# First attention with one set of row statistics ahead of its loop; expert sums scattered into two arrays that are joined at the end, with six buffers for gathered rows

## The chip, the cores and the metric

One core of one Trainium2 chip runs the whole program in one launch. The metric is device time in microseconds (us); lower is better. An engine is called PE (TensorE), PEld (its weight loads), DVE (VectorE), ACT (ScalarE), POOL (GpSimd) or SP (SyncE, which only issues DMAs here).

## The reference, cut to what matters

The input x has 64 sequences of 64 rows of 256 f32 values: T = 4096 rows, held as NT = 32 tiles of 128 rows (two sequences each). Four layers follow one another, each of the form x = x + layer(layernorm(x)):

1. a cross-attention with 32 heads of 8 and rotary positions, on a context of 128 values per row;
2. a feed-forward that keeps half of the rows;
3. a second cross-attention with 16 heads of 16;
4. a mixture of 64 experts, 8 chosen per row, at most 64 rows per expert:

```
w, sel = top_k(softmax(x @ gate_w.T), 8);  w = w / sum(w)
xin[e, slot] = x[token]                       (slot < 64, later ones are dropped)
h = silu(xin @ wg[e]) * (xin @ wu[e])
y[token] += (h @ wd[e]) * w                   (every expert adds to its rows)
```

## The kernel before, in words

All data is f32. x stays in SBUF (`k.xres`) through the first three layers. Each layer is a stage with a barrier at its end, and in each stage every engine runs its own list of instructions, tied to the others by semaphores.

**First attention** (`first_attention`). SP issues the constants, a first part of x, the weights, the keys and values of tiles 0 and 1, and then the rest of x. x comes in six parts, `X_PARTS`, of 4, 4, 6, 6, 6 and 6 tiles. DVE takes the layernorm statistics of part 0 alone (`part_statistics(0)`: one `bn_stats` per tile at L469, then five small operations at L108 to L114 for the part), ACT makes the scale (L121, L123), DVE the shift (L129), and the loop over the tiles begins. The loop is a software pipeline of depth 5: step n normalises tile n (L485), makes its query and key (L364, L365), and works on tiles n-1 to n-4 at later points (scores L292 with the maximum and the subtraction L490 and L494 on DVE; transposes L304, exponentials L411, products with the values L316; output L382, residual L509). `pipelined` writes the first steps out (6 on PE and POOL; 8 on ACT and DVE, by `PEEL`) and runs the rest as a loop. On DVE steps 1 to 5 each end with `part_statistics(n)` for the next part of x, ahead of step n+1's normalisation in DVE's order. SP puts three later loads (weights of the other layers) behind the key and value loads of each of tiles 2 to 13.

**Route and slots** (`route`, `fill_slots`). The rows are normalised again, gated, and stored with their 64 expert weights as a table of rows of 320 values in DRAM (`table`, L1151); x itself is stored into `out` (L1147), in eight groups of four tiles. `fill_slots` then finds each expert's rows, with DVE alone busy for most of it.

**Experts** (`experts`). 64 experts are worked through as 32 pairs, two pairs to a batch: 16 batches (`NB_E`). Of each pair, POOL gathers 128 rows of the table by an indirect DMA (L1414) into one of `GOT_E` = 4 buffers of a batch each. PE turns them (L1444), multiplies (L1470), turns the hidden values (L1486), multiplies again (L1459), and sums rows that both experts of a pair hold with a matmul (L1479); ACT copies the result to `add`, which has two buffers (L1508). POOL scatters the 128 rows of a pair into `out` by an indirect DMA that adds (L1428). The adding reads and writes rows that another pair may hit too, so each scatter waits until the one before it has landed (`e_added`). POOL's order is: scatter of pair 0, gather of pair 0 of batch n+3, scatter of pair 1, gather of pair 1 of batch n+3. SP loads the weights of eight batches ahead, 1.125 MiB per batch (768 KB and 384 KB), until batch 7 has been worked through.

Of the kernel before, what the change touches and what calls it, by code (L numbers as in the profile page):

```python
# [6 lines left out]
F32 = mybir.dt.float32  # L7
U32 = mybir.dt.uint32
ALU = mybir.AluOpType
# [3 lines left out]
P = 128  # L13
# [39 lines left out]
GOT_E = 4  # L53
# [4 lines left out]
def pipelined(eng, step, tiles, depth, peel=0):  # L58

    first = max(depth + depth % 2, peel)
# [38 lines left out]
def row_statistics(dve, k, done, tiles=slice(0, NT), before=0):  # L104

    raw = k.raw[:, tiles, :]
    mean2, apart, square = k.mean2[:, tiles], k.apart[:, tiles], k.square[:, tiles]
    dve.tensor_tensor(mean2, raw[:, :, 1], raw[:, :, 4], ALU.add).then_inc(done, 1)  # L108
    dve.tensor_tensor(apart, raw[:, :, 1], raw[:, :, 4], ALU.subtract).then_inc(done, 1)
    dve.tensor_tensor(square, raw[:, :, 2], raw[:, :, 5], ALU.add).then_inc(done, 1)  # L110
    dve.wait_ge(done, 5 * before + 2)
    dve.scalar_tensor_tensor(out=k.spread2[:, tiles], in0=apart, scalar=0.25, in1=apart, op0=ALU.mult, op1=ALU.mult).then_inc(done, 1)
    dve.wait_ge(done, 5 * before + 4)
    dve.scalar_tensor_tensor(out=k.var[:, tiles], in0=square, scalar=1.0 / D, in1=k.spread2[:, tiles],  # L114
                             op0=ALU.mult, op1=ALU.add).then_inc(done, 1)


def row_scales(act, k, statistics_done, ln_done, scale_done, tiles=slice(0, NT), before=0):

    act.wait_ge(statistics_done, 5 * before + 5)  # L120
    act.activation(k.lnv[:, tiles], k.var[:, tiles], ACT.Ln, bias=k.ln_eps[:, 0:1]).then_inc(ln_done, 1)  # L121
    act.wait_ge(ln_done, before + 1)
    act.activation(k.rstd[:, tiles], k.lnv[:, tiles], ACT.Exp, scale=-0.5).then_inc(scale_done, 1)  # L123


def row_shifts(dve, k, scale_done, shift_done, tiles=slice(0, NT), before=0):

    dve.wait_ge(scale_done, before + 1)
    dve.scalar_tensor_tensor(out=k.nmr[:, tiles], in0=k.mean2[:, tiles], scalar=-0.5, in1=k.rstd[:, tiles],  # L129
                             op0=ALU.mult, op1=ALU.mult).then_inc(shift_done, 1)  # L130
    dve.wait_ge(shift_done, before + 1)
# [27 lines left out]
def first_attention(nc, ins, k, bank):  # L159

    with ExitStack() as stack:
# [24 lines left out]
        (a_const, a_weights, a_xin0, a_xin1, a_xin2, a_xin3, a_xin4, a_xin5, a_keys0, a_keys1, a_vals0, a_vals1, a_fill, a_ang, a_turns,  # L186
# [4 lines left out]
             "a_const a_weights a_xin0 a_xin1 a_xin2 a_xin3 a_xin4 a_xin5 a_keys0 a_keys1 a_vals0 a_vals1 a_fill a_ang a_turns "  # L191
# [3 lines left out]
        x_in, keys_done, vals_done = [a_xin0, a_xin1, a_xin2, a_xin3, a_xin4, a_xin5], [a_keys0, a_keys1], [a_vals0, a_vals1]  # L195
# [3 lines left out]
        PEEL = 8  # L199
        X_PARTS = [slice(0, 4), slice(4, 8), slice(8, 14), slice(14, 20), slice(20, 26), slice(26, NT)]  # L200
# [14 lines left out]
        def _(sp):  # L215
            def load_x(c):
                sp.dma_start(k.xres[:, X_PARTS[c], :], x_rows[:, X_PARTS[c], :]).then_inc(x_in[c], 16)

# [170 lines left out]
        def _(act):  # L389
# [9 lines left out]
            row_scales(act, k, a_stats, a_lnv_done, a_rstd_done, X_PARTS[0])  # L399

            def step(n, i, u, on):
                t, tk, a, w, f = n, n - 1, n - 2, n - 3, n - 4
                v = 1 - u
                if isinstance(n, int) and 2 <= n <= len(X_PARTS):
                    row_scales(act, k, a_stats, a_lnv_done, a_rstd_done, X_PARTS[n - 1], n - 1)

# [39 lines left out]
            pipelined(act, step, NT, DEPTH, PEEL)  # L446

        @block.vector
        def _(dve):
# [15 lines left out]

            def part_statistics(c):
                dve.wait_ge(x_in[c], 16)
                for t in range(X_PARTS[c].start, X_PARTS[c].stop):
                    dve.bn_stats(tile_of(k.raw, t), tile_of(k.xres, t)).then_inc(a_raw, 1)  # L469
                dve.wait_ge(a_raw, X_PARTS[c].stop)  # L470
                row_statistics(dve, k, a_stats, X_PARTS[c], c)

            part_statistics(0)
            row_shifts(dve, k, a_rstd_done, a_nmr_done, X_PARTS[0])
            dve.wait_ge(a_table, 4)

            def step(n, i, u, on):
                t, a, w, f = n, n - 2, n - 3, n - 4
                v = 1 - u
                if isinstance(n, int) and 3 <= n <= len(X_PARTS) + 1:  # L480
                    row_shifts(dve, k, a_rstd_done, a_nmr_done, X_PARTS[n - 2], n - 2)
# [617 lines left out]
def route(nc, ins, k, bank, out, table):  # L1099
# [4 lines left out]
    with ExitStack() as stack:  # L1104
# [34 lines left out]
        def _(sp):  # L1139
# [3 lines left out]
            sp.dma_start(table[T:T + P, :], zero[:, :]).then_inc(r_pad, 16)  # L1143
            for g in range(groups):
# [9 lines left out]
            sp.wait_ge(r_pad, 32)  # L1154
# [219 lines left out]
def experts(nc, ins, k, bank, out, table):  # L1374

    with ExitStack() as stack:
# [13 lines left out]
        (e_idx_s, e_got0, e_got1, e_got2, e_got3, e_gotT, e_gotTc, e_row, e_twin_s, e_again_s, e_shift_s, e_to_s,  # L1390
         e_gu, e_silu, e_hid_s, e_hidT, e_hidTc, e_y, e_part_s, e_sum, e_add_s, e_added
         ) = z.sems(
             "e_idx_s e_got0 e_got1 e_got2 e_got3 e_gotT e_gotTc e_row e_twin_s e_again_s e_shift_s e_to_s "
             "e_gu e_silu e_hid_s e_hidT e_hidTc e_y e_part_s e_sum e_add_s e_added")
        got_in = [e_got0, e_got1, e_got2, e_got3]
# [13 lines left out]
        def _(pool):  # L1409
# [12 lines left out]
            for n in range(NB_E):  # L1422
                pool.wait_ge(e_to_s, n + 1)
                pool.wait_ge(e_add_s, n + 1)
                for p in range(2):
                    if n or p:
                        pool.wait_ge(e_added, 16 * (2 * n + p))
                    pool.indirect_dma_start(out=out[:, :], out_offset=bass.IndirectOffsetOnAxis(ap=to[:, n, p:p + 1], axis=0),  # L1428
                                            in_=add[:, n % 2, p, :], in_offset=None, compute_op=ALU.add).then_inc(e_added, 16)
# [60 lines left out]
        def _(act):  # L1490
            act.preload_act_table(ACT.Silu)
            for n in range(NB_E + 1):
# [65 lines left out]
def program(nc, ins, out, table):  # L1558
    with ExitStack() as stack:
# [52 lines left out]
        with nc.sbuf_tensor("found", [P, T // 2], F32) as found:  # L1612
            k.found = found
            route(nc, ins, k, bank, out, table)
            fill_slots(nc, ins, k, bank)
        experts(nc, ins, k, bank, out, table)
# [73 lines left out]
```

## Time and profile before

| | before |
|---|---|
| time, median of 3 runs | 1127.8 us (1126.14 to 1131.03) |
| the profiled execution's own time | 1132.87 us |
| its span (first to last instruction) | 1131.1 us |
| busy: PE / DVE / ACT / POOL | 903.2 / 662.7 / 426.4 / 334.1 us |
| mean granted clock of TensorE | 0.887 |
| DMA traffic | 56.28 MB |

The span is what the trace shows; 1.8 us of the execution's time lie around it. A busy share is a mean over stages with different limits, so the stages are read one by one. "xn" below is the normalised tile, and the start of its instruction on DVE marks the start of a step in the first attention.

### The profile page before, as it was taken

What the parts mean: (1) busy time and instruction counts of PE and PEld (TensorE: products, weight loads), DVE (VectorE), ACT (ScalarE), POOL (GpSimd) and SP (SyncE); (2) the same over time, 40 slices, a digit from 0 to 9 for tenths busy, and PEclk for the clock granted to TensorE, in tenths of its full rate; (3) what the DMA queues carried; (4) which work ended last, traced back from release to release, by engine and by line L of the source; (5) the groups of instructions that cost most, each with busy time, mean ns of one, the idle gap of its engine ahead of it and who ended that gap; (6) DMA issues with size and microseconds to landing.
All of it is one profiled execution on the core that took longest, in us unless ns stands there. A gap on an engine that the chain in (4) does not pass through costs nothing. (4 is left out here: it accounts for less than half of the span.)

```text
span 1131.1 us, 25460 instructions
## 1 busy us (share of the span) xinstructions
PE 903.2 (80%) x9176; PEld 693.5 (61%) x9176; DVE 662.7 (59%) x1481; ACT 426.4 (38%) x1013; POOL 334.1 (30%) x293
## 2 busy tenths in 40 slices
PE   4789999999998599998699999999977600655661
PEld 2567777777776598897467777777746500433440
DVE  4756777777775455553377677776742586333331
ACT  2324444444443223333266655656537400221220
POOL 3313333433441200000333333333410101344552
PEclk9678999999999699999699999999985655788886
DMA  6311100000000000000101100001003592567342
GB/s 196 94 35 33 27 14 14 14 14 14 14 9 4 1 1 0 0 0 1 17 16 17 16 14 14 14 16 17 12 1 113 195 297 93 137 174 188 63 68 24
DMA packets 74395, 56.28 MB, mean 50 GB/s; under 512 B 40689, under 2 KB 69489, under 8 KB 74353
## 3 DMA queue, kind: packets, MB, share of 16 engines
q1 hardware_dynamic: 68208, 46.29, 14.0%
q0 software_dynamic: 6144, 9.44, 4.9%
q8 instruction: 25, 0.41, 0.2%
q14 instruction: 18, 0.14, 0.0%
HBM read 41.78 MB, written 13.93 MB: 49 GB/s over the span
## 5 line engine op out<-in xcount | busy, mean ns | idle before, releaser
L411 ACT ACTIVATE pr_t<-bank 128x512 f32<-128x512 f32 x128 | 76.3, 596 | 159.7 <-PE bank L304 159.0
L837 POOL TENSOR_TENSOR g_k_bd<-g_k_t,head_mask 128x1024 f32<-128x1024 f32 x32 | 60.6, 1893 | 133.3 <-ACT g_k_t L1016 133.3
L316 PEld LDWEIGHTS bank<-v_bd,pr_t 128*64 128x64 f32 x2048 | 73.1, 142 | 27.8 <-issue 27.6
L304 PE MATMUL bank<-ident,sub 128*128 128x128 f32 x512 | 86.3, 293 | 3.0 <-ACT pr_t L411 2.3
L316 PE MATMUL bank<-v_bd,pr_t 128*64 128x18 f32 x2048 | 86.0, 217 | 0.1
L304 PEld LDWEIGHTS bank<-ident,sub 128*128 128x128 f32 x512 | 59.7, 147 | 29.6 <-issue 18.6
L494 DVE TENSOR_TENSOR sub<-bank,top 128x2048 f32<-128x2048 f32 x32 | 73.3, 2291 | 3.7
L264 POOL TENSOR_TENSOR rot<-part_a,part_b 128x512 f32<-128x512 f32 x32 | 40.6, 1268 | 116.9 <-DVE part_b L503 116.9
L655 ACT ACTIVATE f_hid<-bank,b 128x128 f32<-128x128 f32 x128 | 36.5, 368 | 97.7 <-PE bank L600 97.7
L490 DVE TENSOR_REDUCE top<-bank 128x32 f32<-128x2048 f32 x32 | 73.1, 2284 | 0.3
L1428 POOL DMA_INDIRECT out<-e_add,e_to x32 | 50.7, 1583 | 75.0 <-DMA out<-e_add,e_to 57.2
L272 POOL TENSOR_TENSOR k_bd<-qk_t,head_mask 128x1024 f32<-128x1024 f32 x32 | 60.6, 1893 | 33.0 <-ACT qk_t L426 33.0
L600 PE MATMUL bank<-f_xs_t,w 128*128 128x128 f32 x512 | 64.5, 280 | 0.0
L600 PEld LDWEIGHTS bank<-f_xs_t,w 128*128 128x128 f32 x512 | 60.4, 194 | 5.1 <-ACT f_hid L655 5.0
L636 PE MATMUL bank<-w,f_hid 128*128 128x256 f32 x256 | 57.9, 379 | 0.0
L986 ACT ACTIVATE g_sq<-g_qk 128x512 f32<-128x512 f32 x32 | 20.2, 630 | 86.9 <-DVE g_qk L1091 86.9
L503 DVE TENSOR_TENSOR part_a<-bank,cos_t 128x512 f32<-128x512 f32 x32 | 22.1, 692 | 52.0 <-PE bank L365 52.0
L636 PEld LDWEIGHTS bank<-w,f_hid 128*128 128x128 f32 x256 | 47.4, 190 | 5.8
L1524 DVE COPY e_part<-bank 128x512 f32<-128x512 f32 x16 | 11.1, 691 | 67.7 <-PE bank L1459 67.7
L1414 POOL DMA_INDIRECT e_got<-table,e_idx x32 | 31.6, 988 | 62.4 <-DVE e_idx L1517 52.9
L1444 PE MATMUL bank<-ident,e_got 128*128 128x128 f32 x64 | 12.3, 322 | 46.1 <-DMA e_got<-table,e_idx 46.1
L980 ACT ACTIVATE g_pr_t<-bank 128x512 f32<-128x512 f32 x64 | 38.2, 597 | 19.1 <-PE bank L881 18.4
(192 smaller groups left out, 2073.8 us busy)
## 6 DMA issues: line engine op xcount, KB each, us to landing
e_w_gu<-in_experts_in SPq DMA_DIRECT2D x16, 768.0 KB, 5.4
e_w_d<-in_experts_out SPq DMA_DIRECT2D x16, 384.0 KB, 6.4
table<-r_row SPq DMA_DIRECT2D x16, 320.0 KB, 2.9
out<-xres SPq DMA_DIRECT2D x16, 256.0 KB, 3.3
xres<-in_x SPq DMA_DIRECT2D x4, 768.0 KB, 9.8
keys_in<-in_ctx_t SPq DMA_DIRECT2D x32, 64.0 KB, 1.9
vals_in<-in_ctx_t SPq DMA_DIRECT2D x32, 64.0 KB, 1.8
w<-in_L_ffn_w SPq DMA_DIRECT2D x2, 1024.0 KB, 6.8
```

The costliest lines, as they stand in the source:

```text
L264: pool.tensor_tensor(rot[:, v, :], part_a[:, v, :], part_b[:, v, :], ALU.add).then_inc(a_rot, 1)
L272: pool.tensor_tensor(k_bd[:, v, :, :, :, :].rearrange("p c b h s -> p (c b) h s"), qk_t[:, v, KC:2 * KC, :].rearrange("p c (b a s) -> p (c ...
L304: m = pe.transpose(b_pr[:, j * P:(j + 1) * P], sub[:, v, cols], k.ident[:, :])
L316: m = pe.matmul(b_o[64 * b:64 * b + 64, hp * VW0:(hp + 1) * VW0], pr_t[:, e, j, b * S:(b + 1) * S], v_bd[:, v, b, hp, :], start=True, stop ...
L411: act.activation(pr_t[:, e, :, :].rearrange("p j q -> p (j q)"), b_pr[:, :], ACT.Exp).then_inc(a_exp, 1)
L490: dve.tensor_reduce(top[:, :], sc, AX.X, ALU.max).then_inc(a_top, 1)
L494: dve.tensor_tensor(sub[:, u, :].rearrange("p (h s) -> p h s", s=S), sc, stretch(top[:, :], S), ALU.subtract).then_inc(a_sub, 1)
L600: mm = pe.matmul(b_h[half][:, (c % 4) * P:(c % 4 + 1) * P], k.w1[:, d, c * P:(c + 1) * P], xs_t[:, u, d, :], start=(d == 0), stop=(d == KC ...
L636: mm = pe.matmul(b_y[:, 0:D], hid[:, u, c, :], k.w2[:, c, :], start=(c == 0), stop=(c == FC - 1))
L837: pool.tensor_tensor(k_bd[:, v, :, :, :, :].rearrange("p c b h s -> p (c b) h s"), k_t[:, v, :, :].rearrange("p c (b a s) -> p (c b) a s", ...
L980: act.activation(pr_t[:, e, :, :].rearrange("p j q -> p (j q)"), b_pr[:, :], ACT.Exp).then_inc(g_exp, 1)
L1428: pool.indirect_dma_start(out=out[:, :], out_offset=bass.IndirectOffsetOnAxis(ap=to[:, n, p:p + 1], axis=0), in_=add[:, n % 2, p, :], in_o ...
```

## The change: what it does

It has two parts that share no code.

**First attention.** x comes in four parts of eight tiles (1 MB each). DVE takes the statistics of all 32 tiles ahead of the first step (four small loops over `bn_stats`, then the five operations, the scale and the shift once, 32 columns wide). No step has statistics in it any more. `PEEL` goes, so that ACT and DVE write out six steps as the others do. All 30 later loads stand right behind x in SP's list, ahead of the keys and values of tile 2.

**Experts.** The scatter of pair 0 of a batch adds to `out`, that of pair 1 to a new DRAM array `extra`; each waits only for the scatter before it on the same array. Both are issued, then the two gathers, now of batch n+5, since `GOT_E` is 6. At the end four DMAs of POOL add `extra` to `out`, DRAM to DRAM, 1 MB each. `extra` has to be zero first: `route` fills it with nine DMAs, 4.3 MB, ahead of its other stores in SP's list.

```
-GOT_E = 4
+GOT_E = 6
...
-            for c in range(1, len(X_PARTS)):
+            for c in range(1, PARTS):
                 load_x(c)
-            ahead, share = 14, -(-len(k.later_loads) // 12)
-            for t in range(2, ahead):
-                both(t, t // 2, t % 2)
-                for dst, src in k.later_loads[(t - 2) * share:(t - 1) * share]:
-                    sp.dma_start(dst, src).then_inc(k.loaded, 16)
-            with sp.Fori(ahead // 2, NT // 2) as i:
+            for dst, src in k.later_loads:
+                sp.dma_start(dst, src).then_inc(k.loaded, 16)
+            with sp.Fori(1, NT // 2) as i:
...
-            part_statistics(0)
-            row_shifts(dve, k, a_rstd_done, a_nmr_done, X_PARTS[0])
+            for c, part_in in enumerate(x_in):
+                dve.wait_ge(part_in, 16)
+                with dve.Fori(c * NT // PARTS, (c + 1) * NT // PARTS) as t:
                     dve.bn_stats(tile_of(k.raw, t), tile_of(k.xres, t)).then_inc(a_raw, 1)
+            dve.wait_ge(a_raw, NT)
+            row_statistics(dve, k, a_stats)
+            row_shifts(dve, k, a_rstd_done, a_nmr_done)
...
-                if isinstance(n, int) and 1 <= n < len(X_PARTS):
-                    part_statistics(n)
-            pipelined(dve, step, NT, DEPTH, PEEL)
+            pipelined(dve, step, NT, DEPTH)
...
+            for c in range(NT // 4):
+                sp.dma_start(extra[4 * P * c:4 * P * (c + 1), :].rearrange("(t p) d -> p t d", p=P),
+                             spread(zero[:, 0:D], 4)).then_inc(r_pad, 16)
+            sp.dma_start(extra[T:T + P, :], zero[:, 0:D]).then_inc(r_pad, 16)
...
-                for p in range(2):
-                    if n or p:
-                        pool.wait_ge(e_added, 16 * (2 * n + p))
-                    pool.indirect_dma_start(out=out[:, :], ..., compute_op=ALU.add).then_inc(e_added, 16)
-                    if n + GOT_E - 1 < NB_E:
-                        gather(n + GOT_E - 1, p)
-            pool.wait_ge(e_added, 32 * NB_E)
+                for p, sum_of, landed in ((0, out, e_added), (1, extra, e_extra)):
+                    if n:
+                        pool.wait_ge(landed, 16 * n)
+                    pool.indirect_dma_start(out=sum_of[:, :], ..., compute_op=ALU.add).then_inc(landed, 16)
+                for p in range(2):
+                    if n + GOT_E - 1 < NB_E:
+                        gather(n + GOT_E - 1, p)
+            pool.wait_ge(e_added, 16 * NB_E)
+            pool.wait_ge(e_extra, 16 * NB_E)
+            for c in range(4):
+                rows = slice(c * T // 4, (c + 1) * T // 4)
+                pool.dma_start(out=out[rows, :]..., in_=extra[rows, :]...,
+                               accum_op=ALU.add, max_dma_last_dim=8192).then_inc(e_joined, 16)
+            pool.wait_ge(e_joined, 64)
...
-                        act.wait_ge(e_added, 32 * (n - 2))
+                        act.wait_ge(e_added, 16 * (n - 2))
+                        act.wait_ge(e_extra, 16 * (n - 2))
```

DVE in step 2 of the first attention, from its normalisation to that of step 3, before (`raw`, `mean`, `apart`, `square`, `spread`, `var` are the statistics, `nmr` the shift, `sub` the scores less their maximum):

```order
L485 TENSOR_SCALAR xn<-xres,rstd,nmr 128x256
L490 TENSOR_REDUCE top<-bank 128x32
L494 TENSOR_TENSOR sub<-bank,top 128x2048
L503 TENSOR_TENSOR part_a<-bank,cos_t 128x512
L503 TENSOR_TENSOR part_b<-bank,sin_t 128x512
L469 BN_STATS raw<-xres 128x6 x6
L108 TENSOR_TENSOR mean<-raw 128x6
L109 TENSOR_TENSOR apart<-raw 128x6
L110 TENSOR_TENSOR square<-raw 128x6
L112 SCALAR_TENSOR_TENSOR spread<-apart 128x6
L114 SCALAR_TENSOR_TENSOR var<-square,spread 128x6
L129 SCALAR_TENSOR_TENSOR nmr<-mean,rstd 128x4
```

The same place in the changed kernel, where its lines have other numbers:

```order
L475 TENSOR_SCALAR xn<-xres,rstd,nmr 128x256
L480 TENSOR_REDUCE top<-bank 128x32
L484 TENSOR_TENSOR sub<-bank,top 128x2048
L493 TENSOR_TENSOR part_a<-bank,cos_t 128x512
L493 TENSOR_TENSOR part_b<-bank,sin_t 128x512
L475 TENSOR_SCALAR xn<-xres,rstd,nmr 128x256
```

The twelve instructions of the statistics that stood between two normalisations are gone from the step; they stand ahead of step 0 now, for all tiles.

POOL at the start of the experts, before (`e_got` are the gathered rows, `e_add` the rows to be added, `e_idx` and `e_to` the row numbers):

```order
L1414 DMA e_got<-table,e_idx 128x320 x6
L1428 DMA out<-e_add,e_to 4224x256
L1414 DMA e_got<-table,e_idx 128x320
L1428 DMA out<-e_add,e_to 4224x256
L1414 DMA e_got<-table,e_idx 128x320
```

and in the changed kernel, its start and its end:

```order
L1406 DMA e_got<-table,e_idx 128x320 x10
L1420 DMA out<-e_add,e_to 4224x256
L1420 DMA extra<-e_add,e_to 4224x256
L1406 DMA e_got<-table,e_idx 128x320 x2
...
L1420 DMA out<-e_add,e_to 4224x256
L1420 DMA extra<-e_add,e_to 4224x256
L1429 DMA out<-extra 128x2048 x4
```

The two scatters of a batch stand side by side, the gathers behind both, ten gathers instead of six come before the first scatter, and the four joining DMAs (128 rows of 2048 values, 8 KB, each) come last.

## Rows read from the trace of the kernel before

**Rows 1.** The page, granted clock of TensorE in 40 slices of 28 us.

```profile
PEclk9678999999999699999699999999985655788886
```

**Rows 2.** DVE's timeline (start us, us, instruction): step starts in the first attention.

```profile
9.69 0.41 DVE L485 TENSOR_SCALAR xn<-xres,rstd,nmr 128x256 f32<-128x256 f32 x1
...
15.62 0.40 DVE L485 TENSOR_SCALAR xn<-xres,rstd,nmr 128x256 f32<-128x256 f32 x1
...
25.21 0.41 DVE L485 TENSOR_SCALAR xn<-xres,rstd,nmr 128x256 f32<-128x256 f32 x1
...
84.12 0.41 DVE L485 TENSOR_SCALAR xn<-xres,rstd,nmr 128x256 f32<-128x256 f32 x1
...
98.42 0.41 DVE L485 TENSOR_SCALAR xn<-xres,rstd,nmr 128x256 f32<-128x256 f32 x1
...
108.03 0.41 DVE L485 TENSOR_SCALAR xn<-xres,rstd,nmr 128x256 f32 x1
```

**Rows 3.** Timeline at the end of step 5: statistics on DVE, then PE's wait.

```profile
81.29 2.05 DVE L469 BATCH_NORM_STATS2 raw<-xres 128x6 f32<-128x256 f32 x6
...
84.67 0.69 PE L332 MATMUL bank<-ident,xn 128*128 128x128 f32 x2 [2.67 <-DVE xn L485]
```

**Rows 4.** PE's timeline, the query product in step 6 and in step 7.

```profile
90.92 2.07 PE L364 MATMUL bank<-wq,xn_t 128*128 128x256 f32 x4
...
102.44 1.13 PE L364 MATMUL bank<-wq,xn_t 128*128 128x256 f32 x4
```

**Rows 5.** Windows (us; busy PE, PEld, DVE, ACT, POOL; clock, DMA share, GB/s).

```profile
20.00:24.00 4.00, 3.41 (x37) 1.77 (x35) 1.97 (x5) 0.00 (x0) 1.52 (x2) 1.00 0.15 50
```

**Rows 6.** Windows in the second attention, whose first step starts at 540.86.

```profile
540.00:550.00 10.00, 5.59 (x14) 3.19 (x14) 3.13 (x6) 1.84 (x5) 2.67 (x6) 0.50 0.09 14
...
560.00:570.00 10.00, 7.96 (x90) 5.70 (x90) 6.03 (x11) 6.05 (x14) 2.62 (x2) 1.00 0.14 23
```

**Rows 7.** POOL's timeline in the experts: first, middle and last scatters.

```profile
974.43 1.62 POOL L1428 DMA_INDIRECT out<-e_add,e_to  x1 [11.10 <-ACT e_add L1508]
...
1036.49 1.59 POOL L1428 DMA_INDIRECT out<-e_add,e_to  x1 [3.32 <-DMA out<-e_add,e_to]
...
1038.39 0.98 POOL L1414 DMA_INDIRECT e_got<-table,e_idx  x1 [0.30 <-issue]
...
1040.60 1.59 POOL L1428 DMA_INDIRECT out<-e_add,e_to  x1 [1.23 <-DMA out<-e_add,e_to]
...
1046.69 1.59 POOL L1428 DMA_INDIRECT out<-e_add,e_to  x1 [3.22 <-DMA out<-e_add,e_to]
...
1121.04 1.55 POOL L1428 DMA_INDIRECT out<-e_add,e_to  x1 [2.49 <-DMA out<-e_add,e_to]
```

**Rows 8.** The chain that ended last: the scatter before the last, from issue to landing.

```profile
1117.00 3.78 DMA out<-e_add,e_to
```

**Rows 9.** The page, costliest groups (count, busy us, mean ns, idle before): the scatters.

```profile
L1428 POOL DMA_INDIRECT out<-e_add,e_to x32 | 50.7, 1583 | 75.0 <-DMA out<-e_add,e_to 57.2
```

**Rows 10.** PE's timeline, turning gathered rows and hidden values in the first batches.

```profile
967.04 0.60 PE L1444 MATMUL bank<-ident,e_got 128*128 128x128 f32 x4
...
973.95 0.60 PE L1444 MATMUL bank<-ident,e_got 128*128 128x128 f32 x4
...
978.91 0.42 PE L1486 MATMUL bank<-ident,e_hid 128*96 128x128 f32 x2 [0.75 <-DVE e_hid L1532]
```

**Rows 11.** Windows: weight loads alone; experts with weight loads; one scatter alone.

```profile
910.00:930.00 20.00, 0.00 (x0) 0.00 (x0) 19.73 (x13) 0.00 (x0) 0.00 (x0) 0.50 0.97 314
1035.00:1045.00 10.00, 6.30 (x36) 3.94 (x36) 3.12 (x12) 1.90 (x4) 5.14 (x4) 0.83 0.64 168
1112.20:1116.90 4.70, 0.00 (x0) 0.00 (x0) 0.00 (x0) 0.00 (x0) 1.55 (x1) 0.50 0.25 28
```

**Rows 12.** SP's timeline in the route stage: the first stores of x, the first of the table.

```profile
848.72 0.98 SPq L1147 DMA_DIRECT2D out<-xres  x2
867.78 0.88 SPq L1151 DMA_DIRECT2D table<-r_row  x2
```

More of the change, by code:

```diff
@@ L52, with pipelined @@
 RING_E = 8
-GOT_E = 4
+GOT_E = 6
 GT = 4
 ROWS_R = 4
-def pipelined(eng, step, tiles, depth, peel=0):
-    first = max(depth + depth % 2, peel)
+def pipelined(eng, step, tiles, depth):
+    first = depth + depth % 2
     def peeled(n):
@@ L101, in stretch @@
     return ap.rearrange("p (h a) -> p h a", a=1).to_broadcast([ap.shape[0], ap.shape[1], n])
[L104 to L114, printed above, removed]
-                             op0=ALU.mult, op1=ALU.add).then_inc(done, 1)
@@ L118, in row_scales, with row_statistics @@
[L118 to L129, printed above, removed]
+def row_statistics(dve, k, done):
+    mean_e, mean_o = k.raw[:, :, 1], k.raw[:, :, 4]
+    dve.tensor_tensor(k.mean2[:, :], mean_e, mean_o, ALU.add).then_inc(done, 1)
+    dve.tensor_tensor(k.apart[:, :], mean_e, mean_o, ALU.subtract).then_inc(done, 1)
+    dve.tensor_tensor(k.square[:, :], k.raw[:, :, 2], k.raw[:, :, 5], ALU.add).then_inc(done, 1)
+    dve.wait_ge(done, 2)
+    dve.scalar_tensor_tensor(out=k.spread2[:, :], in0=k.apart[:, :], scalar=0.25, in1=k.apart[:, :],
+                             op0=ALU.mult, op1=ALU.mult).then_inc(done, 1)
+    dve.wait_ge(done, 4)
+    dve.scalar_tensor_tensor(out=k.var[:, :], in0=k.square[:, :], scalar=1.0 / D, in1=k.spread2[:, :],
+                             op0=ALU.mult, op1=ALU.add).then_inc(done, 1)
@@ L130, in row_shifts, with row_scales @@
+def row_scales(act, k, statistics_done, ln_done, scale_done):
+    act.wait_ge(statistics_done, 5)
+    act.activation(k.lnv[:, :], k.var[:, :], ACT.Ln, bias=k.ln_eps[:, 0:1]).then_inc(ln_done, 1)
+    act.wait_ge(ln_done, 1)
+    act.activation(k.rstd[:, :], k.lnv[:, :], ACT.Exp, scale=-0.5).then_inc(scale_done, 1)
+def row_shifts(dve, k, scale_done, shift_done):
+    dve.wait_ge(scale_done, 1)
+    dve.scalar_tensor_tensor(out=k.nmr[:, :], in0=k.mean2[:, :], scalar=-0.5, in1=k.rstd[:, :],
                              op0=ALU.mult, op1=ALU.mult).then_inc(shift_done, 1)
-    dve.wait_ge(shift_done, before + 1)
+    dve.wait_ge(shift_done, 1)
@@ L445, in step @@
                                    ACT.Copy).then_inc(a_attTc, 1)
-            pipelined(act, step, NT, DEPTH, PEEL)
+            pipelined(act, step, NT, DEPTH)
         @block.vector
@@ L1095, in second_attention, with route @@
         z.end()
-def route(nc, ins, k, bank, out, table):
+def route(nc, ins, k, bank, out, extra, table):
     with ExitStack() as stack:
@@ L1370, in fill_slots, with experts @@
         z.end()
-def experts(nc, ins, k, bank, out, table):
+def experts(nc, ins, k, bank, out, extra, table):
     with ExitStack() as stack:
@@ L1555, in over_rows, with program @@
     return vector.rearrange("(a d) -> a d", a=1).to_broadcast([rows, vector.shape[0]])
-def program(nc, ins, out, table):
+def program(nc, ins, out, extra, table):
     with ExitStack() as stack:
@@ L1613, in program @@
             k.found = found
-            route(nc, ins, k, bank, out, table)
+            route(nc, ins, k, bank, out, extra, table)
             fill_slots(nc, ins, k, bank)
-        experts(nc, ins, k, bank, out, table)
+        experts(nc, ins, k, bank, out, extra, table)
 def shape_constants():
@@ L1685 @@
     out = nc.dram_tensor("out", [T + P, D], F32, kind="ExternalOutput").ap()
+    extra = nc.dram_tensor("extra", [T + P, D], F32, kind="Internal").ap()
     table = nc.dram_tensor("table", [T + P, ROW], F32, kind="Internal").ap()
-    program(nc, ins, out, table)
+    program(nc, ins, out, extra, table)
     r = run_bass_kernel_spmd(nc, [arrays], core_ids=[0])
```

40 lines of the change are left out of this document (16 added, 24 removed).

## The prediction

> **What bounds the kernel now.** I read the page first. PE is busy through most slices, but two places stand out [rows 1]: the granted clock is 0.6 to 0.8 in slices 2 to 4, the first attention's start, and 0.5 to 0.8 in the last ten slices, route to experts. The change touches these two, and the route stage between them only by stores. So I read three timelines.
>
> In the first attention, steps start at 9.69, 15.62 and 25.21, and step 8 at 108.03, while a step without statistics at full clock takes 108.03 - 98.42 = 9.6 us [rows 2]. Why the early ones are long shows at step 6: DVE takes six tiles' statistics first (2.05 us, and 84.12 - 81.29 = 2.8 with the small operations), and PE sits idle 2.67 us until DVE has normalised the next tile [rows 2, 3]. After that wait PE works at half speed: the same four matmuls take 2.07 us in step 6 and 1.13 in step 7 [rows 4]. So a statistics block costs its own 2.8 us and then a stretch at 1.2 GHz: step 6, cold and with no statistics behind it, takes 98.42 - 84.12 = 14.3 us, 4.7 more than a warm one [rows 2].
>
> In the experts the bound is a chain of scatters. Pair 0 to pair 1 takes 1040.60 - 1036.49 = 4.1 us, pair 1 to the next pair 0 6.1, a batch 10.2 [rows 7]. From 1046.69 to 1117.00 eight batches take 8.8 us each, with the weights loaded [rows 7, 8]. POOL's scatter itself is 1.58 us [rows 9] and a gather 0.98 after a gap of 0.30 [rows 7]; the rest is waiting for the landing, 3.78 us from issue [rows 8]. PE could go faster: a batch takes 978.91 - 973.95 = 5.0 us from turning the rows to turning the hidden values, so about 5.4 to the next batch, and 973.95 - 967.04 = 6.9 when part of it is cold [rows 10].
>
> **First attention, the cost.** Step 0 must now wait for all of x. In the window from 20 to 24 us the DMA engines are busy 0.15, 0.6 us of it [rows 5]: the loading ends at about 20.6, and x is its last large part. The bytes ahead of it stay the same, so x is complete then. Eight `bn_stats` of the last part (2.05 / 6 = 0.34 each [rows 3], 2.7), 0.8 for the small operations as in step 6, and 0.8 for ACT's scale, which now lies on the path, give a first step at about 24.9 instead of 9.69: **+15.2**. At least +13 (x at 19), at most +18 (loop overhead of the 32 `bn_stats`, which no row prices).
>
> **First attention, the gain.** Steps 0 to 7 take 98.3 us now. Without statistics steps 0 and 1 take 5.9 and 9.6 - 2.1 = 7.5, since step 1's block is four tiles long. Step 2 I put at 8.0, step 3 at 9.5 (both fill the pipeline and have less to do than a full step), and steps 4 to 7 at 9.6 each: 69.3, so -29.0 if PE is warm from step 2 on. The second attention has its statistics ahead already, and there the clock is 0.50 in the first 10 us and 1.00 from 20 us on, with nothing that cools it again [rows 6]. PE starts cold here too; I allow one more half-cold step, 2.6: **-26.4**, with ends of -29 and -17 (two cold steps more). Net for the stage: **-11.2**, from -16 to +1. The rest of the stage is bound by PE at full clock and doesn't change. The later loads, 30 DMAs of about 3.6 MB behind x, land by some 32 us, and the keys of tile 2, queued behind them, are needed by step 2 at about 43 us: nothing. The missing peel: nothing, the same instructions in a loop.
>
> **Route.** Nine more DMAs, 4 us of SP's issuing and 4.3 MB, go out at 848. SP's first stores of x stand there, but nothing waits for them, and the first table rows are ready only at 867.8 [rows 12]; at the plain rate of 314 GB/s [rows 11] the zeros need 13.7 us, and SP issues nothing else between 850 and 867.8. I take **+0.5**, for instruction loads that share the engines; ends 0 and +3.
>
> **Experts, the batches.** POOL's own work per batch is two scatters and two gathers, 2 x 1.58 + 2 x 0.98, four gaps of 0.3 and 0.5 at the turn: 6.9 us. The landing (3.78) hides in it, since the next scatter on the same array comes a whole batch later. The DMA engines are the other limit: they are busy 0.64 of a 10.2 us batch now, 6.5 us [rows 11], while weights are loaded, so that a 6.9 us batch would keep them 94% busy. I take 7.5 us for those eight batches. Three more have gathers, 6.9 each. The last have none, 4.2 us of POOL, and PE sets 5.4. With the first scatter at 974.4 as now [rows 7]: 974.4 + 60 + 20.7 + 4 x 5.4 = 1076.7, and the last pair lands 1.9 + 3.8 behind, 1082.4. Now it is 1121.04 + 3.8 = 1124.8: **-42.4**, ends -48 (6.9 everywhere) and -30 (9 us with weights). Six buffers cost nothing: ten gathers at 1.28 us, from 956 on, end before the first result at 973.
>
> **Experts, the join.** New at the end, with no cover: `extra` read, `out` read and written, 4.2 MB each. No row shows a DRAM-to-DRAM add, so I bound it. Below: the plain rate, each byte once, 4.2 MB / 314 GB/s = 13.4 us [rows 11]. Above: a scatter of 128 KB keeps the DMA engines 0.25 x 4.7 = 1.2 us busy [rows 11], 32 of them 38 us. The scatter moves 1 KB pieces and the join 8 KB pieces, as the weight loads about do, so I am nearer the plain rate; but two sources must be read, twice 13.4 = 26.8. With 2.6 us for issue and landing (3.8 - 1.2): **+29.4**, ends 16 and 41.
>
> The Trainium skill (Collectives: The Full Stack, section on the fold count and why AG ≠ RS ≠ AR) says a DMA add runs at half of a copy's rate because each chunk is read from two sources through one ring, at about 31 GB/s per engine for a copy. That is the doubling taken above; by its figure 16 engines would give 248 GB/s, an estimate of 17 us for the data of the join, and the sum would come out 10 us lower. No trace here shows such an add.
>
> **The sum.** -11.2 + 0.5 - 42.4 + 29.4 = -23.7. Against the profiled execution's 1132.9 that is 1109.2. That execution lies 5.1 above the median of the three runs, 1127.8, and so I forecast 1104. All good ends together (-16, 0, -48, +16) give 1080, all bad ones (+1, +3, -30, +41) 1143; not all fall on one side, and I take 1086 to 1128.
>
> **The rivals.**
>
> A, *each piece of the join waits for the one before it on its engine* (slower). For: from the end of a scatter's issue to its landing 2.2 us pass for 8 KB per engine; if the adding DMA takes that long per piece of 8 KB, 32 pieces per engine take 70 us. Against: the engines are busy only 1.2 us of it, and six gathers already overlap. It decides once the join costs more than 53 us. Time: 1104 + 41 = 1145. Chance 0.07.
>
> B, *DMA engines become the bound in the batches with weights*. For: 94% busy in the sum. Against: the weights may lag several batches without anybody waiting. If those eight batches stay at 10.2: 1104 + 8 x 2.7 = 1126. Chance 0.06.
>
> C, *the clock stays low in the first attention*, because the late start leaves PE idle for 25 us. For: short matmuls with gaps in the first steps. Against: the second attention recovers [rows 6]. Four cold steps more at 4.7: 1104 + 19 = 1123. Chance 0.06.
>
> D, *two scatters in flight take as long as two in a row*, as both are spread over the same engines. Against: an engine share of 0.25 leaves room for a second [rows 11]. The batches would then gain nothing: 1104 + 42 = 1146. Chance 0.02. The Trainium skill (DMA: Bandwidth & Descriptors, Rules for kernel authors) says that transfers to two disjoint halves serialise and that several queues buy no bandwidth. By that rule, D; the share in the trace speaks against it.
>
> **How the numbers follow.** My case has 0.79. A measurement of this kernel can tell about 0.5%, 5.6 us, from no change. Faster by more: 0.79 and half of C, 0.82. Within 0.5%: B and the other half of C, 0.09. Slower: A and D, 0.09. The range leaves out A, D and the tails of my own case.
>
> **What would show it.** First xn at 24 to 26 us, step starts then 9.6 to 10 us apart from step 4 on, no PE wait over 1 us for xn, clock 1.00 by 45 us: right. Scatters to `out` 7 to 8 us apart, then 5 to 6; the last at 1065 to 1072 (the stage begins 10 us earlier). A join of 27 to 32 us from the last landing. Wrong would be a join beyond 41 us, scatters over 9 us apart, or a gathered row that PE waits for.

## The result, and the profile after

| | before | after |
|---|---|---|
| time, median (lowest to highest), 4 runs each | 1129.41 us (1126.14 to 1134.07) | 1097.18 us (1096.58 to 1099.33) |
| ratio to before, 95% interval | | 0.9715 (0.9676 to 0.9754) |
| the profiled execution: time, span | 1132.87, 1131.1 us | 1099.33, 1097.6 us |
| mean granted clock | 0.887 | 0.899 |

The change is faster by 2.85%, inside the forecast range and 6.8 us below the forecast. The table goes through the program by the two traces (us; a stage's end is the next stage's start):

| | before | after | difference | forecast |
|---|---|---|---|---|
| start of step 0, first attention | 9.69 | 29.65 | +20.0 | +15.2 |
| steps 0 to 7 | 98.3 | 71.1 | -27.3 | -26.4 |
| start of step 8 | 108.03 | 100.73 | -7.3 | -11.2 |
| first gather of the experts issued | 955.87 | 948.90 | -7.0 | -10.7 |
| first gather to the last scatter's landing | 168.9 | 118.7 | -50.2 | -42.4 |
| join, from that landing | 0 | 23.2 | +23.2 | +29.4 |
| from there to the end of the span | 6.3 | 6.8 | +0.5 | 0 |

The last row but one ends with the landing of the last joining DMA: it is issued at 1069.9 and lands 20.9 us later, at 1090.8. The profiled execution is the slowest of the changed kernel's four, 2.2 us above their median.

The page after, the granted clock in 40 slices of 27.4 us; against [rows 1] the second, third and fourth digits have risen from 6, 7, 8 to 8, 9, 9, and the last five, from 960 us on, are 9, 8, 9, 7 for the batches and 5 for the join:

```profile
PEclk9899999999999699999699999999997555598975
```

DVE's timeline after, at the start, answers to [rows 2]:

```profile
8.83 3.89 DVE L463 BATCH_NORM_STATS2 raw<-xres  x8 [3.10 <-DMA xres<-in_x]
16.20 11.68 DVE L463 BATCH_NORM_STATS2 raw<-xres  x24 [3.48 <-DMA xres<-in_x]
...
29.65 0.41 DVE L475 TENSOR_SCALAR xn<-xres,rstd,nmr 128x256 f32<-128x256 f32 x1
...
43.20 0.40 DVE L475 TENSOR_SCALAR xn<-xres,rstd,nmr 128x256 f32<-128x256 f32 x1
...
61.33 0.40 DVE L475 TENSOR_SCALAR xn<-xres,rstd,nmr 128x256 f32<-128x256 f32 x1
...
100.73 0.41 DVE L475 TENSOR_SCALAR xn<-xres,rstd,nmr 128x256 f32 x1
```

The last 24 `bn_stats` run without a gap, at 11.68 / 24 = 0.487 us each. In [rows 3] one takes 0.34, written out; here it stands in a loop. From step 4 on a step takes (100.73 - 61.33) / 4 = 9.85 us.

Windows after (columns as in [rows 5]): the first attention, the batches with weights and without, and the join.

```profile
44.00:48.00 4.00, 1.67 (x15) 1.05 (x14) 3.97 (x2) 1.75 (x4) 3.26 (x3) 0.88 0.00 0
48.00:52.00 4.00, 4.00 (x30) 2.53 (x38) 1.80 (x4) 0.00 (x0) 0.04 (x1) 0.50 0.14 37
52.00:56.00 4.00, 4.00 (x54) 2.97 (x38) 3.56 (x4) 1.95 (x4) 2.83 (x3) 0.77 0.00 0
56.00:60.00 4.00, 3.89 (x54) 3.17 (x50) 2.59 (x3) 1.97 (x4) 1.12 (x1) 1.00 0.11 33
970.00:980.00 10.00, 8.94 (x72) 6.24 (x72) 5.92 (x24) 3.34 (x8) 6.81 (x6) 1.00 1.07 310
1030.00:1040.00 10.00, 8.28 (x70) 5.85 (x70) 5.74 (x23) 3.43 (x8) 8.17 (x7) 1.00 0.51 95
1070.00:1080.00 10.00, 0.00 (x0) 0.00 (x0) 0.00 (x0) 0.00 (x0) 1.67 (x2) 0.50 0.97 197
1080.00:1088.00 8.00, 0.00 (x0) 0.00 (x0) 0.00 (x0) 0.00 (x0) 0.00 (x0) 0.50 1.03 214
```

After PE's light window from 44 us (1.67 of 4 us busy) one stretch is cold: the clock is 0.88, 0.50 and 0.77 in the three windows, which comes to some 7 us at the lower level, and from 56 us it is full. While weights are loaded the DMA engines are full (a share of 1.07 against 0.64 in [rows 11]), and without weights half busy.

POOL's timeline after answers to [rows 7]: a batch with weights whose scatter waited, one without, the last ones, and the join.

```profile
987.33 1.62 POOL L1420 DMA_INDIRECT out<-e_add,e_to  x1 [0.42 <-DVE e_to L1547]
991.82 1.58 POOL L1420 DMA_INDIRECT extra<-e_add,e_to  x1 [2.86 <-DMA extra<-e_add,e_to]
...
1024.22 1.63 POOL L1420 DMA_INDIRECT out<-e_add,e_to  x1 [0.30 <-issue]
...
1030.65 1.61 POOL L1420 DMA_INDIRECT out<-e_add,e_to  x1 [0.30 <-DVE e_hid L1532]
1032.57 1.57 POOL L1420 DMA_INDIRECT extra<-e_add,e_to  x1 [0.30 <-issue]
1034.44 1.02 POOL L1406 DMA_INDIRECT e_got<-table,e_idx  x1 [0.30 <-DMA out<-e_add,e_to]
1035.77 0.98 POOL L1406 DMA_INDIRECT e_got<-table,e_idx  x1 [0.30 <-issue]
1037.06 1.63 POOL L1420 DMA_INDIRECT out<-e_add,e_to  x1 [0.30 <-issue]
...
1043.48 1.61 POOL L1420 DMA_INDIRECT out<-e_add,e_to  x1 [0.30 <-issue]
...
1061.96 1.55 POOL L1420 DMA_INDIRECT out<-e_add,e_to  x1 [1.18 <-DMA out<-e_add,e_to]
...
1068.19 3.48 POOL L1429 DMA_DIRECT2D out<-extra  x4 [2.82 <-DMA extra<-e_add,e_to]
```

The first scatter stands at 965.78. Eight batches to 1024.22 take 7.3 us each, three to 1043.48 take 6.4, and four to 1061.96 take 4.6. In the middle stretch POOL never pauses by more than 0.3 us: two scatters, two gathers and four gaps are 6.4 us, and POOL is the bound. In the last four batches a scatter waits for the one before it on its own array (3.8 us from issue to landing, 0.8 to the next issue).

The chain after shows the longest landing in the batches with weights and the very last one:

```profile
982.72 8.83 DMA extra<-e_add,e_to
...
1063.82 3.78 DMA extra<-e_add,e_to
```

A scatter lands in 3.78 us alone, as in [rows 8], and in up to 8.83 us where the engines are full. Who waits for that shows in the waits after, from 940 us on (total us, times, longest):

```profile
ACT e_add L1508 <- DMA extra<-e_add,e_to: 20.1, 6, 7.2
...
PE bank L1443 <- DMA e_got<-table,e_idx: 7.6, 1, 7.6
POOL out L1420 <- DMA out<-e_add,e_to: 7.4, 6, 1.7
```

PE waits for gathered rows once, at the start. The same view of before, from 955 us on, has a line that the prediction didn't read:

```profile
PE bank L1444 <- DMA e_got<-table,e_idx: 46.1, 14, 7.6
```

### The profile page after: what moved, and what is told of

It is laid out like the page before. It is cut to its first block and busy times, and to the rows that moved or that the text cites. A ratio compares the mean times of both kernels' runs of the same rounds, so it can differ in the third digit from the quotient of the medians.

```text
span 1097.6 us, 25638 instructions
## 1 busy us (share of the span) xinstructions
PE 879.1 (80%) x9176; PEld 678.4 (62%) x9176; DVE 662.9 (60%) x1451; ACT 422.4 (38%) x1003; POOL 338.4 (31%) x297
## 5 line engine op out<-in xcount | busy, mean ns | idle before, releaser
L313 PEld LDWEIGHTS bank<-v_bd,pr_t 128*64 128x64 f32 x2048 | 70.0, 137 | 26.6 <-issue 26.4
L301 PE MATMUL bank<-ident,sub 128*128 128x128 f32 x512 | 82.8, 284 | 3.0 <-ACT pr_t L406 2.3
L313 PE MATMUL bank<-v_bd,pr_t 128*64 128x18 f32 x2048 | 82.8, 214 | 0.1
L301 PEld LDWEIGHTS bank<-ident,sub 128*128 128x128 f32 x512 | 56.2, 141 | 30.8 <-issue 17.6
L264 POOL TENSOR_TENSOR xres<-xres,bo 128x256 f32 (+1 forms) x32 | 23.4, 730 | 78.0 <-DVE xn L475 78.0
L493 DVE TENSOR_TENSOR part_a<-bank,cos_t 128x512 f32<-128x512 f32 x32 | 22.1, 692 | 38.0 <-PE bank L362 38.0
L881 PEld LDWEIGHTS bank<-g_v_bd,g_pr_t 128*64 128x64 f32 x1024 | 35.3, 136 | 15.7 <-issue 15.7
```

The source lines that it names most:

```text
L301: m = pe.transpose(b_pr[:, j * P:(j + 1) * P], sub[:, v, cols], k.ident[:, :])
L313: m = pe.matmul(b_o[64 * b:64 * b + 64, hp * VW0:(hp + 1) * VW0], pr_t[:, e, j, b * S:(b + 1) * S], v_bd[:, v, b, hp, :], start=True, stop ...
```

## The experiments

Runs with the same time of before in the table shared one chip, so their ratios compare directly. Two kernels ran once and have no interval.

| run | median us | before us | ratio (95%) |
|---|---|---|---|
| attention only | 1121.21 | 1131.95 | 0.9905 (0.9888 to 0.9921) |
| experts only | 1103.43 | 1131.95 | 0.9754 (0.9735 to 0.9772) |
| experts, statistics in the gap | 1083.86 | 1131.95 | 0.9579 (0.9550 to 0.9607) |
| changed, no join | 1072.28 | 1129.96 | 0.9489 (0.9454 to 0.9523) |
| changed, four buffers | 1125.55 | 1129.96 | 0.9966 (0.9939 to 0.9993) |
| changed, statistics written out | 1092.86 | 1129.96 | 0.9667 (0.9638 to 0.9695) |
| changed, loads spread | 1096.05 | 1129.96 | 0.9683 (0.9652 to 0.9714) |
| changed, join by a plain copy | 1087.44 | 1127.66 | one run |
| changed, join in 1 KB pieces | 1097.03 | 1127.66 | one run |
| small blocks in the gap | 1079.28 | 1131.69 | 0.9558 (0.9525 to 0.9590) |
| before, six buffers | 1132.94 | 1131.69 | 1.0022 (1.0000 to 1.0045) |
| changed, five buffers | 1097.16 | 1131.69 | 0.9731 (0.9676 to 0.9785) |

### Each half alone

The first kernel has the changed first attention, and route and experts as before; the second the reverse.

> The first attention of the change, the route and the experts of before. My theory (the two parts share nothing): xn starts at 29.6 us as in the changed kernel, step 8 at 100.7, the rest as before; 7 us under the kernel before, 1122. Rival (the later loads, issued at once, or the earlier route also matter further on): a difference that is not near 7, or stages behind it that last longer than before.

> The first attention of before, the zeros, experts and join of the change. My theory: batches 50 us shorter, join 24 us, route 1 us longer, so 25 to 26 us under the kernel before, about 1104. Rival (the gain needs the other part): off by more than 3 us from the sum, which says that the two parts add up to 32.

Attention alone gives -10.7 us and experts alone -28.5. The first half repeats in its trace: step 0 starts at 29.74 and step 8 at 100.87, as in the changed kernel. The second half's kernel has before's first attention, and yet in its profiled execution step 8 starts at 98.98 where [rows 2] have 108.03, with the clock at 0.91 and 0.92 from 40 to 60 us where before's trace has 0.67. That execution took 1096.6 us, the kernel's other three 1101.9 to 1105.5. So the cold steps of before differ from execution to execution, by up to 9 us, and what the attention half gives depends on the execution that it is set against. By the medians the two halves don't add up: -10.7 and -28.5 are 39.2 us, while the whole change gives 32.2, and 33.9 and 34.5 in the two kernels below that equal it (loads spread, five buffers). So beside the experts' half the attention half is worth some 4 to 6 us and not 10.7; no run here shows why. The changed kernel's own step starts agree with those of the attention-only run within 0.6 us, but they aren't fixed either: the five-buffer and no-join kernels have the same attention, and their steps 0 to 7 take 68.9 and 68.8 us in place of 71.1.

### The start: the loop, and the loads behind x

```
-                with dve.Fori(c * NT // PARTS, (c + 1) * NT // PARTS) as t:
+                for t in range(c * NT // PARTS, (c + 1) * NT // PARTS):
                     dve.bn_stats(tile_of(k.raw, t), tile_of(k.xres, t)).then_inc(a_raw, 1)
```

> The changed kernel with the 32 statistics instructions ahead of the first attention written out in place of four loops. My theory (a loop iteration costs 0.49 us and the instruction 0.34): 0.15 us less for each of the 24 last, first xn at 26 to 27 instead of 29.6, 2.5 to 3.5 us less in all. Rival (the loading of x sets the start, and the loop hides behind it): first xn stays past 29.

DVE's timeline of this run:

```profile
22.14 2.71 DVE L463 BATCH_NORM_STATS2 raw<-xres 128x6 f32<-128x256 f32 x8 [0.28 <-DMA xres<-in_x]
24.88 0.21 DVE L107 TENSOR_TENSOR mean<-raw 128x32 f32<-128x32 f32 x1
...
26.62 0.41 DVE L475 TENSOR_SCALAR xn<-xres,rstd,nmr 128x256 f32<-128x256 f32 x1
```

A `bn_stats` takes 2.71 / 8 = 0.34 again, the first step starts 3.0 us earlier and step 8 at 97.68, and the median is 3.2 us below that of the loads-spread kernel (below) on the same chip. The last part of x now shows its landing, 22.1 us. The prediction had it at 20.6.

The other run puts the later loads back among the key and value loads of tiles 2 to 13, as before had them.

> The changed kernel with the 30 later loads issued three per tile as before. My theory: x is ahead of them in the queue, so the first xn does not move and the time is within 1.5 us. Rival (they take DMA time from the last part of x): first xn earlier by 1 us or more.

The first step starts at 29.38 and the time is 1096.05 us: the place of the later loads is worth nothing that shows in the time. It does show in the DMA engines. Their windows in this run, then in the written-out kernel, which has the loads right behind x:

```profile
20.00:21.00 1.00, 0.00 (x0) 0.00 (x0) 0.87 (x3) 0.00 (x0) 0.00 (x0) 1.00 0.20 71
21.00:22.00 1.00, 0.00 (x0) 0.00 (x0) 0.87 (x3) 0.00 (x0) 0.00 (x0) 1.00 0.00 0
```

```profile
20.00:21.00 1.00, 0.00 (x0) 0.00 (x0) 1.00 (x4) 0.00 (x0) 0.00 (x0) 1.00 1.12 406
```

With the loads spread the engines have moved the last of x soon after 20 us, as the prediction read it from the kernel before. With the loads right behind x they stay full, and x lands at 22.1. So it is the later loads that hold x back, by about 1 us or more, though they are issued behind it. In the changed kernel the loop over `bn_stats` hides that. A kernel with the loop written out and the loads spread, which should start sooner by that much again, was not run.

### The buffers

```
-GOT_E = 6
+GOT_E = 4
```

> The changed kernel with four buffers of gathered rows (two batches less ahead). My theory (POOL's own work paces the batches, gathers are ahead in any case): within 3 us of the changed kernel. Rival (the depth of the gathers lets PE run on while the DMA engines are full): 5 to 15 us slower, with PE waiting for e_got in more than three batches.

This was the largest miss of the study: 1125.55 us, 28 above the changed kernel and 29.5 above the loads-spread kernel on the same chip. Its scatters to `out` stand at 984.49, 990.90, 1002.05, 1008.48 and 1019.38: two batches take 17.5 us. The timeline of this kernel, POOL and PE, over one such pair:

```profile
984.49 1.62 POOL L1420 DMA_INDIRECT out<-e_add,e_to  x1 [5.10 <-issue]
...
988.29 1.02 POOL L1406 DMA_INDIRECT e_got<-table,e_idx  x1 [0.31 <-issue]
989.62 0.98 POOL L1406 DMA_INDIRECT e_got<-table,e_idx  x1 [0.30 <-issue]
...
1002.05 1.63 POOL L1420 DMA_INDIRECT out<-e_add,e_to  x1 [4.60 <-issue]
```

```profile
993.87 1.12 PE L1443 MATMUL bank<-ident,e_got 128*128 128x128 f32 x4 [4.47 <-DMA e_got<-table,e_idx]
```

This is a loop. The scatters of batch 2 (984.49) are followed by the gathers of batch 5 (988.29, 989.62); PE turns batch 5 at 993.87; in PE's order the sums of batch 4 come behind that, ACT copies them at 1000.67, and the scatter of batch 4 goes out at 1002.05. So 17.5 us carry two batches with four buffers; they would carry three with five buffers (5.9 us a batch) and four with six (4.4 us). POOL needs 6.4, so five should do as well as six. Two more runs test that:

> The changed kernel with five buffers of gathered rows. My theory: with four, the loop from a batch's sums over its scatters, the gathers behind them, their landing and PE's next sums takes 17.6 us and carries two batches, 8.8 each; with five the same loop carries three, 5.9 each, which is under POOL's own 6.4, so the time is within 3 us of six buffers. Rival (the sixth buffer carries the weight phase, when landings take 6 us and more): 6 us or more above it, with PE waiting for e_got several times.

> The kernel before with six buffers of gathered rows and nothing else. My theory (one array, so each scatter waits for the landing of the last, 8.8 to 10.2 us per batch): within 6 us of the kernel before, and batches with weights still 10 us apart. Rival (the buffers alone are the gain, since with four of them the two arrays gave nothing): 20 us or more under the kernel before.

Five buffers give 1097.16 us, the same as six, with scatters 6.4 us apart without weights; from 955 us on PE waits there for gathered rows six times, 12.1 us in all, off the path. Six buffers in the kernel before, with one array, give nothing (1.0022). PE's waits for gathered rows go from 14 (46.1 us) to the one at the start (7.6 us), yet the batches stay at 10.3 us with weights and 8.7 without, and the waits of that run show what holds them:

```profile
ACT e_add L1508 <- DMA out<-e_add,e_to: 62.8, 14, 7.5
...
POOL out L1428 <- ACT e_add L1508: 42.9, 15, 6.0
...
POOL out L1428 <- DMA out<-e_add,e_to: 29.0, 15, 3.0
```

Neither half of the experts' change pays alone. With four buffers the two arrays, their join included, bring 4.4 us even with the new attention's gain in it (0.9966), less than that attention alone (0.9905): the arrays without buffers cost about 6 us net. In the four-buffer trace the stretch from the first gather to the last scatter's landing does shrink, from 168.9 to 148.2 us, but the join takes more than that back. With six buffers it is 118.7. Together, the join paid, the two bring 28.5 (experts only).

### The join

The first kernel leaves out the four joining DMAs.

> The changed kernel without the four joining DMAs; the sums in extra are left out of the result. My theory: the join costs what the trace shows from the last landing to its own, so 23 to 25 us less, 1073 to 1074. Rival (part of that time is an end that any last DMA has): 19 to 21 less.

It takes 1072.28 us, 23.8 less than the loads-spread kernel and 20.6 less than the written-out one, both on the same chip; the former is the one that equals the changed kernel. The trace's 23.2 from landing to landing agrees with that. The four executions of each kernel lie up to 5.8 us apart, so the medians alone would not rule out the rival's 21. The next kernel copies `extra` over `out` without `accum_op`, and the one after it has pieces of 1 KB, as the scatters have, instead of 8 KB.

> The changed kernel with the joining DMAs as plain copies of extra over out (the sums in out are left out of the result). Theory of the prediction (the add reads two sources, a copy one): the four DMAs take about half of the 23 us, 13 us with issue and landing, so 9 to 11 us less, and some 300 to 330 GB/s. Rival (the rate is set by DRAM-to-DRAM traffic or by the pieces, not by the second source): 20 to 23 us, as with the add.

> The changed kernel with the join cut into pieces of 1 KB in place of 8 KB. Theory (the upper end of the prediction, from a scatter of 1 KB rows that keeps the engines busy 1.2 us per 128 KB): 38 us for the join, 15 us slower. Rival (the add costs by the byte, the scatter's share is start-up): 22 to 26 us, within 3 us of the changed kernel.

The joining DMAs in the traces of the changed kernel, of the copy and of the join in 1 KB pieces. Each pair of lines has the starts of the first and the last issue, and how long a DMA takes from its issue to its landing; the shortest is the first DMA's, the longest the last one's:

```profile
L1429 POOL DMA_DIRECT2D out<-extra x4: 937/1312/1776, 1068.2 to 1069.9; - x4
...
DMA to landing us min/median/max: 7.9/14.3/20.9
```

```profile
L1429 POOL DMA_DIRECT2D out<-extra x4: 517/537/630, 1063.5 to 1065.2; - x4
...
DMA to landing us min/median/max: 6.1/10.2/13.6
```

```profile
L1429 POOL DMA_DIRECT2D out<-extra x4: 1403/2126/2942, 1063.7 to 1066.1; - x4
...
DMA to landing us min/median/max: 9.6/16.4/23.0
```

From POOL's first issue to the last landing the adding join takes 22.6 us, the copy 15.3 and the join in small pieces 25.4. The first landing has the fixed part in it; from there the other three DMAs of 1 MB need 14.7, 9.2 and 15.8 us, that is 4.9, 3.1 and 5.3 us each. So adding costs 1.6 times a copy per MB and 1.48 times with the fixed part, and pieces eight times smaller cost 8% more per MB, 12% in all. The copy lies between its theory (13 us) and its rival (20 to 23), nearer the theory. The bound from the scatter's share of the engines (38 us) is refuted. The copy and the small pieces were each executed once.

### The statistics in DVE's gap

Since one cold step is worth more than a statistics block, I asked whether the blocks must go ahead at all. This kernel is the experts-only one, with x in six parts as before. The block of the next part is moved within its step: from the step's end to behind the subtraction, where DVE waits for PE's query.

```
                     dve.tensor_tensor(sub..., b_s..., top..., ALU.subtract)
+                if isinstance(n, int) and 1 <= n < len(X_PARTS):
+                    part_statistics(n)
...
-                if isinstance(n, int) and 1 <= n < len(X_PARTS):
-                    part_statistics(n)
```

> As the experts alone, but in the first attention each part's statistics stand on DVE behind the subtraction of the scores and ahead of its wait for the query product, where it idled 4.8 us, and no longer ahead of the next normalisation. My theory (a statistics block costs PE a wait, and the wait costs it the clock): first xn at 9.7 as before, steps 4 to 7 of 9.6 to 10 us, step 8 at about 81, so 27 us under the experts alone, 1077. Rival (the early steps are slow because PE starts cold or because of the x and later loads under way): step 8 stays at 100 or later and the gain is under 8 us.

19.6 us less than experts-only by the medians, with the same instructions. Step 8 starts at 89.55, 9.4 us sooner than in that kernel's trace; the two profiled executions lie 12.4 us apart, and the rest of the 19.6 is in executions that left no trace. One step is still cold: PE waits 1.76 us for step 4's tile, and a window behind it stands at half clock:

```profile
43.77 0.44 PE L332 MATMUL bank<-ident,xn 128*128 128x128 f32 x2 [1.76 <-DVE xn L485]
```

```profile
48.00:52.00 4.00, 4.00 (x25) 3.05 (x24) 2.81 (x12) 0.73 (x2) 0.00 (x0) 0.50 0.28 74
```

Step 4 takes 58.53 - 43.30 = 15.2 us. The next kernel makes the blocks smaller where the gap is short, in seven parts, each block one step earlier:

```
-        X_PARTS = [slice(0, 4), slice(4, 8), slice(8, 14), slice(14, 20), slice(20, 26), slice(26, NT)]
+        X_PARTS = [slice(0, 4), slice(4, 8), slice(8, 18), slice(18, 22), slice(22, 26), slice(26, 29), slice(29, NT)]
...
-                if isinstance(n, int) and 1 <= n < len(X_PARTS):
-                    part_statistics(n)
+                if isinstance(n, int) and 0 <= n < len(X_PARTS) - 1:
+                    part_statistics(n + 1)
```

> As the statistics in the gap, but in seven parts whose big block (ten tiles) stands in step 1, where DVE waits 6 us, and the later blocks have three or four tiles (2.1 us at most). My theory (the gap of a step at full clock is 2 us, so that blocks of 2.8 us still made PE wait 1.8 and cost step 4 its clock): no step of steps 4 to 7 over 11 us, step 8 at 81 to 84 instead of 89.6, about 6 us less, 1078. Rival (the one cold step comes by itself after the fill, whatever DVE does): one step of 14 us or more again and no gain over 3 us.

1079.28 us, the fastest version here: 4.4% below before, and 1.6% below the five-buffer kernel on the same chip (1097.16), which equals the changed one. Of those 17.9 us, 16.3 are there at step 8 by the two traces. Its windows in the first attention:

```profile
30.00:40.00 10.00, 9.78 (x119) 6.82 (x117) 9.05 (x15) 3.99 (x9) 3.90 (x3) 0.84 0.66 227
40.00:50.00 10.00, 8.63 (x135) 6.90 (x135) 9.79 (x21) 4.89 (x13) 3.89 (x3) 1.00 0.15 38
```

DVE works through 9.05 and 9.79 of 10 us, the clock is full from 40 us on, step 0 starts at 9.10 and step 8 at 82.13.

## Why the prediction was right, step by step

**What bounds the kernel: right, with one line unread.** The steps behind a statistics block were cold, and moving the blocks (the same work), with their sizes changed, removes those from step 4 on; the scatters were the experts' chain. But the chain had a second loop close behind it, through the gathers, and 46 us of PE's waits for it stood in the trace of before.

**Start of step 0: mis-sized, +20.0 for +15.2.** The term "2.05 / 6 = 0.34 each" took the price of a written-out instruction for one in a loop, where it is 0.49. That is 3.0 us, by the written-out kernel. There 1.7 us remain, and 1.5 of them are x, which lands at 22.1 instead of 20.6 for the most part because the later loads, put at nothing, share the engines with it. The stated end of +18 was too tight.

**Steps 0 to 7: right, -27.3 for -26.4, in part by luck.** One half-cold stretch was allowed, and one is there. But the 98.3 us of before that both numbers start from is one execution's; with the 89.6 of the experts-only trace the gain would be 18.5. The missing peel shows no cost. Net of both terms the attention gives 3.9 us less than forecast in this trace.

**Route: right in size.** The experts' first gather comes 7.0 us earlier where step 8 comes 7.3 earlier, so the 4.3 MB of zeros cost little, though SP took 10.5 us to issue them and not 4. From the first store of the route (839.71, for 847.83 before) to the gather it takes 1.1 us more than before, but that is this execution's own: the ten other traces with the zeros have 106.1 to 108.2 us there, the three without them 106.1 to 108.1. So no cost of the zeros shows.

**The batches: right in mechanism, mis-sized by 7.8 us (-50.2 for -42.4).** With weights 7.3 us for 7.5, so 1.6 in all. With gathers only 6.4 for 6.9, 1.4 in all, because the turn of POOL's order costs one gap of 0.3 and not 0.8. Without gathers 4.6 for 5.4, 3.1 in all: PE doesn't set the pace there, though I had put it so. Its own pace was about as put (5.2 us from batch to batch where it doesn't wait, for 5.4), but it had turned batch 12 at 1031.12, 17 us ahead of that batch's scatter at 1048.20, where 12.4 were enough for batch 0 (953.35 to 965.78). POOL had fallen behind PE and drained what had piled up at the pace of the same-array landings. The first scatter comes 16.9 us after the first gather instead of 18.6, which I had left as it was: 1.7. In the batches with weights the DMA engines were as full as foreseen (1.07 for 94%).

**"Six buffers cost nothing": the step that failed as reasoning.** The sentence asked what they cost, not what they buy. I had the arrays down for the whole gain, and expected the four-buffer kernel within 3 us of the changed one. It lost 28 us. The forecast came out all the same because the change had both.

**The join: mis-sized, +23.2 for +29.4.** The doubling for two source reads was too much. The copy took 15.3 us, near the plain rate of [rows 11] (13.4 for the data and 2.6 for issue and landing), and the add 1.6 times the copy's time per MB. The Trainium skill (Collectives: The Full Stack, on the fold count) has a reduction at half of a copy's rate, measured in a ring between cores; the add on one core here runs at 0.63 of the copy's.

**The rivals.** A fell: four joining DMAs of 32 pieces per engine took 23.2 us, not 70. B fell in its number but not its place: the engines are the limit of those eight batches, which take 7.3 us and not 10.2, and landings of 8.8 us hold ACT's copy for 20 us. C fell: step 4 to step 8 run at 9.85 us. D fell: two scatters are in flight in every batch and a batch takes 6.4 us. The Trainium skill (DMA: Bandwidth & Descriptors, Rules for kernel authors) says that transfers to two disjoint partition halves serialise, as both spread over the same engines; the prediction carried that over to two arrays in DRAM. Where the engines are half idle (0.51 in the windows after) two adding scatters do overlap, by these runs.

**The signs.** Of the signs of being right, several failed while the time came out: the first xn at 29.65 and not 24 to 26, a PE wait for xn of 1.71 us at step 1, the full clock from 56 us and not 45, the last scatter to `out` at 1061.96 and not 1065 to 1072, a join of 23.2 and not 27 to 32. Steps 9.6 to 10 us apart from step 4 on held, and so did scatters 7 to 8 us apart with weights (7.3 in the mean). Of the signs of being wrong one shows, in a harmless place: PE waits for a gathered row once, 7.6 us at the start, which before has too (its longest of 14).

All terms: -7.3 + 0.3 - 50.2 + 23.2 + 0.5 = -33.5, for -23.7 forecast, and -33.5 is what the two spans show; the medians differ by 32.2. The join's error and the batches' went the same way, and the start's the other, which is luck: without the start's 4.8 the sum would be 14.6 us off and not 9.8.

**What stays open.** Why some executions of the kernel before have warmer early steps. Which event decides the cold stretch at 48 us of the changed kernel: PE waited 1.71 us for a tile at 36 us and stayed warm, while 1.76 us at 44 us in the gap kernel went with the fall. And why the two halves give less together than apart.

## What to carry to other kernels

When a serial chain is cut, look in the waits for the loop that comes second, and work out how many items it carries per turn: here buffers less two, over 17.5 us. The buffers and the cut pay only together. And work that stalls another engine need not be moved ahead of a loop, where it delays the start by its whole length and by the load that it needs: put it into a gap of the engine that does it, in blocks no longer than the gap (here 1079 us against 1097).

## What the runs showed of the hardware

- Four adding DMAs of 1 MB from DRAM to DRAM take 22.6 us, four plain ones 15.3, with pieces of 8 KB; per MB behind the first landing 4.9 and 3.1 us. With pieces of 1 KB the adding ones take 25.4 us, 5.3 per MB.
- Two adding scatters of 128 rows run beside each other. Each lands in 3.8 us where the engines are free, and in up to 8.8 us beside weight loads that fill them.
- A `bn_stats` of 0.34 us takes 0.49 us in a hardware loop of one instruction on DVE.
- Loads issued behind x in the same queue hold back its landing, by about 1 us or more here (engines done with x soon after 20 us, or x landed at 22.1).
- The same first-attention code, with the clock between its two levels in the early steps, took 89.6 us to step 8 in one execution (experts only) and 98.3 us in another (before).
